# The router's bias, copied by ScalarE into the PSUM banks in place of two bias matmuls per plane

## The chip, the cores and the metric

The kernel runs on one core of one Trainium2 chip. A core has TensorE (PE, matmuls; PEld is its weight load), VectorE (DVE), ScalarE (ACT), GpSimd (POOL) and SyncE (SP, here only a queue that issues DMAs). The engines run at the same time and wait for each other by semaphores. PE writes its products to PSUM, eight banks of 512 fp32 columns on 128 partitions; ACT and DVE can read and write PSUM. The metric is the device time of one execution in microseconds (us).

## What is computed

The input is x, 4096 tokens of 512 values. A first layer (an adaptor per subject and a gated FFN with ternary weights) gives `x1`; a linear layer with a low-rank adaptor gives `h`. The last layer is a mixture whose router chooses two experts of eight for each token and each of the 512 output channels:

```
logits = (h @ router_w.T + router_b).reshape(T, O, E)
probs = softmax(logits);  w, sel = top_k(probs, 2);  w = w / sum(w)
c = zeros((T, E)).at[t_idx, sel].add(w)
expert_out = einsum('th,eoh->teo', h, expert_w) + expert_b
final = einsum('te,teo->to', c, expert_out)
```

The change concerns `+ router_b`, one value for each channel and expert.

## The kernel before

The program has three stages, one after the other. In the first, PE makes `x1` and `h` in 8 blocks of 512 tokens; `h` is written to HBM as a high and a low part (fp32 split in two for the precision of fp32r). The router stage takes 32 tiles of 128 tokens, the expert stage the same 32 tiles once more.

**Router stage.** A tile has two halves `s` of 256 channels (`HO`), a half has four planes `b`, and a plane is one PSUM bank with the logits of 128 tokens, 256 channels and two experts. `router` on PE makes a plane in this way: wait for `evac` (the bank's old contents are read), two products that put the bias into the bank (line 1248: `pick` is a 64-row matrix that selects the rows of one expert, `bias_mm` holds the bias's high part in rows 0 to 7 and its low part in rows 32 to 39), then twelve products of 512 columns (lines 1251 to 1253: four parts `c` of the depth, each high x high, low x high, high x low). The last one counts up `plane_filled`. Behind plane 1 of each half PE runs `codes` for the half before the last: eight products of 256 columns that turn eight sign maps into one code (line 1231); they wait for `signs`.

**ACT** (`router`, `evacuate`, `stand`) takes each filled bank to `L` in SBUF (line 649). Behind the fourth plane of a half stands `stand` of the half before: Sign and Relu over 2048 elements (lines 657, 659), which wait for `tour` and give `signs`. ACT executes in order.

**DVE** (`half`) starts when all four planes of a half are in `L`: it finds the first and second largest of eight (lines 945 to 963), subtracts the second from all (968, 969, counted as `tour`), and in between decodes the code of the half before (909, 913, 918), for which it waits for `code_done`. In the last tiles of the stage (27 to 30) it also sums the weights of tiles 0 and 1, two sums per half (line 1001).

**SP** loads the next tile's `h` (`load_h`) and stores the results.

**Start of the stage.** When the first stage's last gate product is drained, SP loads the bias and then the router's weights, 8 x 1 MB (lines 384 to 387). ACT splits each weight (`split_router`, line 620: high part), DVE makes the low part. On ACT the first split stands ahead of the `x1` store and of the two `turn` copies, for which PE's `adapt` (line 1164) waits by way of DVE. ACT and DVE also split the bias (633, 634, 892), POOL builds `pick`. PE may start plane 0 when the weights of its two experts are split; ACT's first evacuation stands behind its last split.

**End of the stage.** `eraw`, the experts' weights, lies where the router's did, so each pair of loads waits for a plane of the last half. ACT and DVE split them, DVE three of them ahead of its last `half` (line 1024).

The order of every engine's instructions is written out by hand. The part of the code that the change touches:

Of the kernel before, what the change touches and what calls it, by code (L numbers as in the profile page):

```python
# [20 lines left out]
F32 = mybir.dt.float32  # L21
F32R = mybir.dt.float32r
# [3 lines left out]
ALU = mybir.AluOpType  # L26
# [81 lines left out]
def build(nc, x, idx7, idx6, cond_w, w_ffn, WcT, AT, Bt, scal, rwT, rb, ewT, eb, out):  # L108
# [6 lines left out]
    with root:  # L115
        def sb(name, shape, dt, ctx=root):
            return ctx.enter_context(nc.sbuf_tensor(name, shape, dt))
# [71 lines left out]
        p2 = ExitStack()  # L189
        HO = D // 2  # L190

        bias_mm = sb("bias_mm", [64, D], F32R, p2)
        pick = sb("pick", [64, E, P], F32R, p2)
        scratch = ExitStack()
        bias_raw = sb("bias_raw", [64, D], F32, scratch)
        pick_f = sb("pick_f", [64, E, P], F32, scratch)
        scratch.close()
        wts = sb("wts", [P, 2, 2, D], F32, p2)
        pow_id = sb("pow_id", [P, E, P], BF16, p2)
        one_col = sb("one_col", [P, 1], F32, p2)  # L200
# [72 lines left out]
        rhi = sem("rhi")  # L273
        rlo = sem("rlo")
        braw_in = sem("braw_in")
        bzero = sem("bzero")
        bhi = sem("bhi")
        blo = sem("blo")
        b_const = sem("b_const")
        pick0 = sem("pick0")  # L280
        pick_ready = sem("pick_ready")
        hb_in = [sem("hb_in0"), sem("hb_in1")]
        plane_filled = sem("plane_filled")
        evac = sem("evac")
# [60 lines left out]
        def _(sp):  # L345
# [35 lines left out]


            sp.wait_ge(drained, use(NBLK - 1, f"gu{HC - 1}")[0] + 1)
            sp.dma_start(bias_raw[0:E, :], rb).then_inc(braw_in, 16)
            sp.dma_start(bias_raw[32:32 + E, :], rb).then_inc(braw_in, 16)
            for e in range(E):
                sp.dma_start(rraw[:, e, :, :], RWT[e]).then_inc(rraw_in[e], 16)
                if e == 3:
# [75 lines left out]
        @block.gpsimd  # L464
        def _(pool):
            nc.gpsimd.iota(adapter_i[:, :], pattern=[[0, 1]], base=0, channel_multiplier=1).then_inc(consts, 1)
            nc.gpsimd.memset(ident[:, :], 0.0).then_inc(ident_ready, 1)
            pool.wait_ge(ident_ready, 1)
            nc.gpsimd.affine_select(out=ident[:, :], in_=ident[:, :], compare_op=ALU.not_equal, fill=1.0,
                                    base=0, pattern=[[-1, P]], channel_multiplier=1).then_inc(ident_ready, 1)  # L470
            nc.gpsimd.memset(minus_half[:, :], -0.5).then_inc(ident_ready, 1)
            pool.wait_ge(ident_ready, 3)

            def power(i):
                pool.wait_ge(drained, use(i + 1, "ss")[0] + 1)
# [10 lines left out]
            pool.wait_ge(drained, use(NBLK - 1, f"gu{HC - 1}")[0] + 1)  # L486
            nc.gpsimd.memset(pick_f[:, :, :], 0.0).then_inc(pick0, 1)
            for r in range(2):
                pool.wait_ge(pick0, r + 1)
                nc.gpsimd.affine_select(out=pick_f[:, :, :], in_=pick_f[:, :, :], compare_op=ALU.not_equal, fill=1.0,  # L490
                                        base=-32 * r, pattern=[[-1, E], [0, P]], channel_multiplier=1).then_inc(pick0, 1)
            pool.wait_ge(pick0, 3)
            nc.gpsimd.tensor_copy(pick[:, :, :], pick_f[:, :, :]).then_inc(pick_ready, 1)


        @block.scalar
        def _(act):
# [130 lines left out]
            split_router(2)  # L628
            split_router(3)
            adapt(NBLK - 1)  # L630
            act.wait_ge(braw_in, 32)
            act.wait_ge(bzero, 1)
            nc.scalar.activation(bias_mm[0:E, :], bias_raw[0:E, :], ACT.Copy).then_inc(bhi, 1)
            nc.scalar.activation(bias_mm[32:32 + E, :], bias_raw[32:32 + E, :], ACT.Copy).then_inc(bhi, 1)
            copy_h(NBLK - 1, 0)
            send_h(NBLK - 1, 0)
            copy_h(NBLK - 1, 1)
# [2 lines left out]
            for e in range(5, E):  # L640
                split_router(e)
            act.wait_ge(b_const, 1)
            act.wait_ge(h_stored, 16 * 4 * 2 * NBLK)

            def evacuate(n, s, planes=range(4)):

                for b in planes:
                    act.wait_ge(plane_filled, n * PT + (4 * s + b + 1))
                    nc.scalar.activation(L[:, s, 2 * b:2 * b + 2, :], plane[b][:, :, :], ACT.Copy).then_inc(evac, 1)  # L649

            def stand(n, s):

# [15 lines left out]
            def weigh(n, u, trip):  # L668
# [4 lines left out]
                nc.scalar.activation(wts[:, u, 0, :], lead_in[:, u, :], ACT.Sigmoid).then_inc(w_ready, 1)  # L673
                nc.scalar.activation(wts[:, u, 1, :], lead_in[:, u, :], ACT.Sigmoid, scale=-1.0).then_inc(w_ready, 1)  # L674

            router(0, 0)
            router(1, 1)
            router(2, 0)
# [46 lines left out]
        def _(dve):  # L725
# [152 lines left out]
                                        ALU.subtract).then_inc(rlo, 1)  # L878

            finish(NBLK - 1)  # L880
            nc.vector.memset(bias_mm[:, :].bitcast(F32), 0.0).then_inc(bzero, 1)
            turn(NBLK - 1, 0)
            turn(NBLK - 1, 1)
            split_router(0)
# [6 lines left out]
            dve.wait_ge(bhi, 2)  # L891
            nc.vector.tensor_tensor(bias_mm[32:32 + E, :], bias_raw[32:32 + E, :], bias_mm[32:32 + E, :].bitcast(F32),
                                    ALU.subtract).then_inc(blo, 1)
            split_h(NBLK - 1, 0)
            split_router(3)
            split_h(NBLK - 1, 1)
# [187 lines left out]
        def _(pe):  # L1084
# [134 lines left out]

            pe.wait_ge(drained, A_USES - 1)  # L1220
            pe.wait_ge(b_const, 1 + E)
            pe.wait_ge(blo, 1)
            pe.wait_ge(pick_ready, 1)

            def codes(n, s):

# [8 lines left out]
            def router(n, u, trip, first=False):  # L1235
                for s in range(2):
                    o = slice(s * HO, (s + 1) * HO)
                    for b in range(4):
                        if s == 0 and b == 0:
                            pe.wait_ge(hb_in[u], trip * 16 + 16)  # L1240
                        if first and s == 0 and b == 2:
                            pe.wait_ge(drained, A_USES)
                        if first and s == 0:
                            pe.wait_ge(rlo, 2 * b + 2)
                        else:
                            pe.wait_ge(evac, n * PT + (4 * s + b - 3))
                        for r in range(2):
                            mm(plane[b][:, r, :], pick[:, 2 * b + r, :], bias_mm[:, o], start=(r == 0), stop=False)  # L1248
                        w = slice(2 * b, 2 * b + 2)
                        for c in range(DC):  # L1250
                            mm(plane[b][:, :, :], hb[:, u, c, 0, :], rw_hi[:, w, c, o], start=False, stop=False)  # L1251
                            mm(plane[b][:, :, :], hb[:, u, c, 1, :], rw_hi[:, w, c, o], start=False, stop=False)  # L1252
                            last = mm(plane[b][:, :, :], hb[:, u, c, 0, :], rw_lo[:, w, c, o], start=False, stop=(c == DC - 1))  # L1253
# [77 lines left out]
```

## Time and profile before

| | us |
|---|---|
| median of 3 runs | 2628.39 |
| lowest, highest | 2623.78, 2628.57 |
| span of the profiled execution | 2620.5 |
| busy in it: PE, DVE, ACT, POOL | 2539.7, 1777.4, 808.8, 13.0 |
| first plane product, last plane product (start) | 972.5, 1898.9 |

For the profiled execution the page gives only the span, from its first to its last instruction; no time of its own is given. Busy shares say how much an engine has to do, not whether it is waited for; PE's products overlap in the pipeline, so that a product of 0.39 us can start 0.23 us behind the one before. What a plane costs is therefore read from start to start.

### The profile page before, as it was taken

What the parts mean: (1) busy time and instruction counts of PE and PEld (TensorE: products, weight loads), DVE (VectorE), ACT (ScalarE), POOL (GpSimd) and SP (SyncE); (2) the same over time, 40 slices, a digit from 0 to 9 for tenths busy, and PEclk for the clock granted to TensorE, in tenths of its full rate; (3) what the DMA queues carried; (4) which work ended last, traced back from release to release, by engine and by line L of the source; (5) the groups of instructions that cost most, each with busy time, mean ns of one, the idle gap of its engine ahead of it and who ended that gap; (6) DMA issues with size and microseconds to landing.
All of it is one profiled execution on the core that took longest, in us unless ns stands there. A gap on an engine that the chain in (4) does not pass through costs nothing.

```text
span 2620.5 us, 31962 instructions
## 1 busy us (share of the span) xinstructions
PE 2539.7 (97%) x11312; PEld 2004.8 (77%) x11312; DVE 1777.4 (68%) x2719; ACT 808.8 (31%) x984; POOL 13.0 (0%) x20
## 2 busy tenths in 40 slices
PE   5799999999999989999999999999979999999999
PEld 3578888888888867777777777777768888888887
DVE  7973433434344356666676767668889999999995
ACT  5642332323233243434444444444430000000000
POOL 0000000000000000000000000000000000000000
PEclk9999999999999999999999999999989999999999
DMA  4221112111120151111001000100252222222220
GB/s 139 89 93 33 50 32 66 53 45 50 32 66 32 48 183 34 49 40 40 32 32 47 33 32 32 48 32 32 90 181 74 72 72 72 73 74 73 72 73 27
DMA packets 102054, 160.45 MB, mean 61 GB/s; under 512 B 11634, under 2 KB 44914, under 8 KB 101890
## 3 DMA queue, kind: packets, MB, share of 16 engines
q1 hardware_dynamic: 51378, 103.37, 11.5%
q10 hardware_dynamic: 50640, 56.63, 6.7%
q8 instruction: 18, 0.29, 0.0%
q14 instruction: 18, 0.15, 0.0%
HBM read 109.64 MB, written 50.33 MB: 61 GB/s over the span
## 4 chain that ended last, share of the span: by engine, by line
PE 93%; DVE 3%; ACT 1%; issue 1%; SPq 1%; DMA 1%; ACTq 0%; POOL 0%; DVEq 0%; POOLq 0%
PE slot L1125 17%; PE plane L1251 11%; PE plane L1252 9%; PE plane L1253 9%; PE pj L1135 8%; PE ex L1284 8%; PE ex L1286 8%; PE ex L1285 8%; PE plane L1248 4%; PE slot L1175 3%; PE code L1231 2%; PE slot L1101 1%; PE slot L1164 1%; PE slot L1154 1%; DVE acc L1045 0%
## 5 line engine op out<-in xcount | busy, mean ns | idle before, releaser
L1251 PE MATMUL plane<-rw_hi,hb 128*128 128x512 f32 x1024 | 429.7, 420 | 0.0
L1284 PE MATMUL ex<-ew_hi,hb 128*128 128x512 f32 x1024 | 401.1, 392 | 12.8 <-DVE ew_lo L1024 10.4
L1125 PE MATMUL slot<-y_hi,wgu 128*128 128x512 f32 x1024 | 403.5, 394 | 9.6 <-ACT wpj L526 9.6
L1252 PE MATMUL plane<-rw_hi,hb 128*128 128x512 f32 x1024 | 401.4, 392 | 0.0
L1125 PE MATMUL slot<-y_lo,wgu 128*128 128x512 f32 x1024 | 400.8, 391 | 0.0
L1285 PE MATMUL ex<-ew_hi,hb 128*128 128x512 f32 x1024 | 400.1, 391 | 0.0
L1286 PE MATMUL ex<-ew_lo,hb 128*128 128x512 f32 x1024 | 400.1, 391 | 0.0
L1253 PE MATMUL plane<-rw_lo,hb 128*128 128x512 f32 x1024 | 399.9, 390 | 0.0
L649 ACT ACTIVATE L<-plane 128x512 f32<-128x512 f32 x256 | 151.4, 592 | 522.3 <-PE plane L1253 522.1
L1001 DVE SCALAR_TENSOR_TENSOR lead_in<-code_in,wts 128x1024 bf16<-128x1024 bf16 x256 | 311.2, 1216 | 1.2 <-ACT wts L674 0.2
L789 DVE TENSOR_TENSOR hid<-gate,slot 128x512 f32<-128x512 f32 x128 | 87.9, 687 | 259.2 <-ACT gate L535 259.0
L1251 PEld LDWEIGHTS plane<-rw_hi,hb 128*128 128x128 f32 x1024 | 192.3, 188 | 67.7 <-issue 0.2
L1284 PEld LDWEIGHTS ex<-ew_hi,hb 128*128 128x128 f32 x1024 | 193.4, 189 | 54.7 <-issue 9.9
L1125 PEld LDWEIGHTS slot<-y_hi,wgu 128*128 128x128 f32 x1024 | 193.7, 189 | 52.9 <-issue 5.0
L1253 PEld LDWEIGHTS plane<-rw_lo,hb 128*128 128x128 f32 x1024 | 192.8, 188 | 43.8
L1125 PEld LDWEIGHTS slot<-y_lo,wgu 128*128 128x128 f32 x1024 | 193.4, 189 | 40.4
L1285 PEld LDWEIGHTS ex<-ew_hi,hb 128*128 128x128 f32 x1024 | 193.5, 189 | 40.2
L1286 PEld LDWEIGHTS ex<-ew_lo,hb 128*128 128x128 f32 x1024 | 193.2, 189 | 40.5
L1252 PEld LDWEIGHTS plane<-rw_hi,hb 128*128 128x128 f32 x1024 | 193.0, 188 | 31.4
L1135 PE MATMUL pj<-wpj,hid_hi 128*128 128x512 f32 x512 | 206.4, 403 | 1.9 <-DVE hid_lo L795 1.9
L945 DVE TENSOR_TENSOR top<-L 128x1024 f32<-128x1024 f32 x64 | 78.4, 1225 | 187.0 <-ACT L L649 187.0
L673 ACT ACTIVATE wts<-lead_in 128x512 f32<-128x512 f32 x32 | 20.2, 632 | 598.0 <-DVE lead_in L1001 583.1
(122 smaller groups left out, 3323.1 us busy)
## 6 DMA issues: line engine op xcount, KB each, us to landing
hb<-h_scratch SPq DMA_DIRECT2D x34, 512.0 KB, 3.3
h_scratch<-ht ACTq DMA_DIRECT2D x64, 256.0 KB, 3.1
hb<-h_scratch ACTq DMA_DIRECT2D x30, 512.0 KB, 3.8
q_raw<-in_w_ffn SPq DMA_DIRECT2D x24, 512.0 KB, 3.5
x_mix<-in_x SPq DMA_DIRECT2D x8, 1024.0 KB, 5.3
x_scratch<-x_res ACTq DMA_DIRECT2D x8, 1024.0 KB, 4.4
rraw<-in_rwT SPq DMA_DIRECT2D x8, 1024.0 KB, 8.0
lead_scratch<-lead SPq DMA_DIRECT2D x32, 256.0 KB, 2.0
```

The source lines that it names most:

```text
L649: nc.scalar.activation(L[:, s, 2 * b:2 * b + 2, :], plane[b][:, :, :], ACT.Copy).then_inc(evac, 1)
L789: nc.vector.tensor_tensor(hid[:, j % 2, :], gate[:, j % 2, :], slot[s % 2][:, 1, :], ALU.mult).then_inc(drained, 1)
L1001: nc.vector.scalar_tensor_tensor(lead_in[:, k % 2, :].bitcast(BF16).rearrange("p (a n) -> p a n", a=2), code_in[:, k % 2, :, :], float(2 * ...
L1125: last = mm(slot[s % 2][:, g, :], wgu[:, c, r * P:(r + 1) * P], y[:, c, :], start=(c == 0 and v == 0), stop=(c == DC - 1 and v == 1))
L1135: last = mm(pj[k][:, :], h[:, j % 2, k * P:(k + 1) * P], wpj[:, j, :], start=(j == 0 and v == 0), stop=(j == HC - 1 and v == 1))
L1248: mm(plane[b][:, r, :], pick[:, 2 * b + r, :], bias_mm[:, o], start=(r == 0), stop=False)
L1251: mm(plane[b][:, :, :], hb[:, u, c, 0, :], rw_hi[:, w, c, o], start=False, stop=False)
L1252: mm(plane[b][:, :, :], hb[:, u, c, 1, :], rw_hi[:, w, c, o], start=False, stop=False)
L1253: last = mm(plane[b][:, :, :], hb[:, u, c, 0, :], rw_lo[:, w, c, o], start=False, stop=(c == DC - 1))
L1284: mm(ex[e][:, :], hb[:, u, c, 0, :], ew_hi[:, e, c, :], start=(c == 0), stop=False)
L1285: mm(ex[e][:, :], hb[:, u, c, 1, :], ew_hi[:, e, c, :], start=False, stop=False)
L1286: last = mm(ex[e][:, :], hb[:, u, c, 0, :], ew_lo[:, e, c, :], start=False, stop=(c == DC - 1))
```

## The change

ACT fills each bank with the bias before PE comes to it, and all twelve products of a plane add onto it.

- The bias is laid out by the host for all 128 partitions, `[128, 2, 8, 256]` fp32, 2 MB. SP loads it to `bias_sb` with one DMA, ahead of the router's weights, where two of 16 KB were.
- `bias_mm`, `pick` and what makes them (one memset and one subtraction on DVE, two copies on ACT, four instructions on POOL) are gone.
- `evacuate` on ACT reads a bank, waits for its own completion (`evac`), and calls `seed`, a copy of 128x512 from `bias_sb` into the same bank, for the other half of the tile. The last half has no seed.
- PE waits for `seeded` where it waited for `evac`; no product of a plane has `start=True` any more.
- The first four seeds stand on ACT behind all its splits of the router's weights.
- `dynamic_dma_scratch_size` falls to 2048, which makes room in SBUF for `bias_sb`.

```
-            sp.dma_start(bias_raw[0:E, :], rb).then_inc(braw_in, 16)
-            sp.dma_start(bias_raw[32:32 + E, :], rb).then_inc(braw_in, 16)
+            sp.dma_start(bias_sb[:, :, :, :], rb).then_inc(braw_in, 16)
...
+            def seed(s, b):
+                nc.scalar.activation(plane[b][:, :, :], bias_sb[:, s, 2 * b:2 * b + 2, :], ACT.Copy).then_inc(seeded, 1)
             def evacuate(n, s, planes=range(4)):
                 for b in planes:
                     act.wait_ge(plane_filled, n * PT + (4 * s + b + 1))
                     nc.scalar.activation(L[:, s, 2 * b:2 * b + 2, :], plane[b][:, :, :], ACT.Copy).then_inc(evac, 1)
+                    if not (isinstance(n, int) and n == NT - 1 and s == 1):
+                        act.wait_ge(evac, n * PT + (4 * s + b + 1))
+                        seed(1 - s, b)
...
+            act.wait_ge(drained, A_USES - 1)
+            seed(0, 0)
+            seed(0, 1)
+            act.wait_ge(drained, A_USES)
+            seed(0, 2)
+            seed(0, 3)
+            act.wait_ge(h_stored, 16 * 4 * 2 * NBLK)
             router(0, 0)
...
                         if first and s == 0:
                             pe.wait_ge(rlo, 2 * b + 2)
-                        else:
-                            pe.wait_ge(evac, n * PT + (4 * s + b - 3))
-                        for r in range(2):
-                            mm(plane[b][:, r, :], pick[:, 2 * b + r, :], bias_mm[:, o], start=(r == 0), stop=False)
+                        pe.wait_ge(seeded, n * PT + (4 * s + b + 1))
```

PE, in the loop over the tiles, at the end of plane 1 with the codes and the start of plane 2. Before:

```order
L1251 MATMUL plane1<-rw_hi,hb 128x512
L1252 MATMUL plane1<-rw_hi,hb 128x512
L1253 MATMUL plane1<-rw_lo,hb 128x512
L1227 REGISTER_ALU
L1231 MATMUL code1<-sgn,pow_id 128x256 [waits code_read,signs]
L1231 MATMUL code1<-sgn,pow_id 128x256 x7
L1246 REGISTER_ALU
L1248 MATMUL plane2<-bias_mm,pick 128x256 [waits evac]
L1248 MATMUL plane2<-bias_mm,pick 128x256
L1251 MATMUL plane2<-rw_hi,hb 128x512
L1252 MATMUL plane2<-rw_hi,hb 128x512
```

Now:

```order
L1231 MATMUL plane1<-rw_hi,hb 128x512
L1233 MATMUL plane1<-rw_hi,hb 128x512
L1235 MATMUL plane1<-rw_lo,hb 128x512
L1211 REGISTER_ALU
L1215 MATMUL code1<-sgn,pow_id 128x256 [waits code_read,signs]
L1215 MATMUL code1<-sgn,pow_id 128x256 x7
L1228 REGISTER_ALU
L1231 MATMUL plane2<-rw_hi,hb 128x512 [waits seeded]
L1233 MATMUL plane2<-rw_hi,hb 128x512
L1235 MATMUL plane2<-rw_lo,hb 128x512
```

The two bias products between the codes and plane 2 are gone, and the wait for `evac` is one for `seeded` on the first product itself.

ACT, in the same loop, at the last two planes of a half and the `stand` that follows. Before:

```order
L649 ACTIVATE L<-plane2 128x512 [waits plane_filled]
L648 REGISTER_ALU
L649 ACTIVATE L<-plane3 128x512 [waits plane_filled]
L653 ISA
L655 ISA [waits tour]
L657 ACTIVATE sgn<-L 128x2048 [waits code_done]
L658 ISA
L659 ACTIVATE sgn<-sgn,one_col 128x2048 [waits signs]
```

Now:

```order
L628 REGISTER_ALU
L629 ACTIVATE L<-plane2 128x512 [waits plane_filled]
L623 ACTIVATE plane2<-bias_sb 128x512 [waits evac]
L628 REGISTER_ALU
L629 ACTIVATE L<-plane3 128x512 [waits plane_filled]
L623 ACTIVATE plane3<-bias_sb 128x512 [waits evac]
L636 ISA
L638 ISA [waits tour]
L640 ACTIVATE sgn<-L 128x2048 [waits code_done]
L641 ISA
L642 ACTIVATE sgn<-sgn,one_col 128x2048 [waits signs]
```

Between each evacuation and what followed it there is now a copy into the bank that waits for the evacuation; Sign and Relu stand behind the fourth of them.

ACT, at the start of the stage, from the split of expert 5's weights. Before:

```order
L572 DMA h_scratch<-ht 128x4x128 x3
L620 ACTIVATE rw_hi<-rraw 128x2048 [waits rraw_in5]
L620 ACTIVATE rw_hi<-rraw 128x2048 [waits rraw_in6]
L620 ACTIVATE rw_hi<-rraw 128x2048 [waits rraw_in7]
L649 ACTIVATE L<-plane0 128x512 [waits plane_filled,h_stored,b_const]
L649 ACTIVATE L<-plane1 128x512 [waits plane_filled]
L649 ACTIVATE L<-plane2 128x512 [waits plane_filled]
```

Now:

```order
L600 ACTIVATE rw_hi<-rraw 128x2048 [waits rraw_in5]
L600 ACTIVATE rw_hi<-rraw 128x2048 [waits rraw_in6]
L600 ACTIVATE rw_hi<-rraw 128x2048 [waits rraw_in7]
L623 ACTIVATE plane0<-bias_sb 128x512 [waits drained,braw_in,b_const]
L623 ACTIVATE plane1<-bias_sb 128x512
L623 ACTIVATE plane2<-bias_sb 128x512 [waits drained]
L623 ACTIVATE plane3<-bias_sb 128x512
L629 ACTIVATE L<-plane0 128x512 [waits plane_filled,h_stored]
L623 ACTIVATE plane0<-bias_sb 128x512 [waits evac]
```

The four first seeds stand behind the last split, and PE's plane 0 waits for the first of them.

## Rows read from the trace of the kernel before

**Rows 1.** The page: shares, by engine, of the chain of work that ended last.

```profile
PE 93%; DVE 3%; ACT 1%; issue 1%; SPq 1%; DMA 1%; ACTq 0%; POOL 0%; DVEq 0%; POOLq 0%
```

**Rows 2.** Windows: length, us busy by engine (instructions), granted clock, DMA share, GB/s.

```profile
1300.00:1500.00 200.00, 200.00 (x891) 146.81 (x890) 136.95 (x222) 84.01 (x83) 0.00 (x0) 1.00 0.10 37
```

**Rows 3.** The page's groups: one activation of 128x512 that reads and writes SBUF.

```profile
L673 ACT ACTIVATE wts<-lead_in 128x512 f32<-128x512 f32 x32 | 20.2, 632 | 598.0 <-DVE lead_in L1001 583.1
```

**Rows 4.** Order of time, PE, router stage: start, us, engine, line, operation.

```profile
1507.06 0.50 PE L1248 MATMUL plane<-bias_mm,pick 64*128 64x256 f32 x2
1507.49 0.50 PE L1251 MATMUL plane<-rw_hi,hb 128*128 128x512 f32 x1
1507.83 0.40 PE L1252 MATMUL plane<-rw_hi,hb 128*128 128x512 f32 x1
...
1510.12 0.39 PE L1253 MATMUL plane<-rw_lo,hb 128*128 128x512 f32 x1
1510.43 0.50 PE L1248 MATMUL plane<-bias_mm,pick 64*128 64x256 f32 x2
```

**Rows 5.** Order of time, PE, expert stage: the first product of two experts in a row.

```profile
2203.54 0.39 PE L1284 MATMUL ex<-ew_hi,hb 128*128 128x512 f32 x1
...
2206.26 0.39 PE L1284 MATMUL ex<-ew_hi,hb 128*128 128x512 f32 x1
```

**Rows 6.** Order of time, PE: code products before a bias product, and before an expert's.

```profile
1502.69 1.05 PE L1231 MATMUL code<-sgn,pow_id 128*128 128x256 bf16 x8
1503.67 0.50 PE L1248 MATMUL plane<-bias_mm,pick 64*128 64x256 f32 x2
...
1905.67 1.03 PE L1231 MATMUL code<-sgn,pow_id 128*128 128x256 bf16 x8 [0.82 <-issue]
1906.46 0.48 PE L1284 MATMUL ex<-ew_hi,hb 128*128 128x512 f32 x1
```

**Rows 7.** Order of time, ACT, router stage: last evacuation of a half, Sign, Relu.

```profile
1510.54 0.60 ACT L649 ACTIVATE L<-plane 128x512 f32<-128x512 f32 x1 [2.78 <-PE plane L1253]
1511.03 1.90 ACT L657 ACTIVATE sgn<-L 128x2048 bf16<-128x2048 f32 x1
1512.97 2.00 ACT L659 ACTIVATE sgn<-sgn,one_col 128x2048 bf16<-128x2048 bf16 x1
```

**Rows 8.** Order of time, DVE, router stage: one half with two sums, and the next.

```profile
1770.37 1.23 DVE L945 TENSOR_TENSOR top<-L 128x1024 f32<-128x1024 f32 x1 [3.24 <-ACT L L649]
...
1777.38 0.42 DVE L909 TENSOR_SCALAR digits<-code 128x256 int32<-128x256 int32 x1 [1.23 <-PE code L1231]
...
1781.17 0.43 DVE L918 TENSOR_SCALAR slot_code<-digits 128x512 uint16<-128x512 uint16 x1
...
1784.77 1.23 DVE L945 TENSOR_TENSOR top<-L 128x1024 f32<-128x1024 f32 x1 [0.76 <-ACT L L649]
```

**Rows 9.** Order of time, ACT and then PE, start of the router stage.

```profile
946.06 1.91 ACT L620 ACTIVATE rw_hi<-rraw 128x2048 fp32r<-128x2048 f32 x1 [5.22 <-DMA rraw<-in_rwT]
...
979.72 5.51 ACT L620 ACTIVATE rw_hi<-rraw 128x2048 fp32r<-128x2048 f32 x3 [2.71 <-issue]
...
954.03 0.47 PE L1164 MATMUL slot<-x1t_hi,a_hi 128*128 128x512 f32 x1 [2.46 <-DVE x1t_lo L826]
...
984.10 0.76 PE L1248 MATMUL plane<-bias_mm,pick 64*128 64x256 f32 x2 [4.75 <-DVE rw_lo L877]
...
992.94 0.50 PE L1248 MATMUL plane<-bias_mm,pick 64*128 64x256 f32 x2
```

**Rows 10.** Windows at the start of the stage.

```profile
944.00:948.00 4.00, 0.00 (x0) 0.00 (x0) 2.84 (x5) 1.91 (x1) 3.43 (x4) 0.98 1.05 401
...
984.00:988.00 4.00, 3.90 (x10) 3.03 (x11) 4.00 (x2) 2.31 (x3) 0.00 (x0) 0.50 0.15 46
```

**Rows 11.** Order of time, PE and then DVE, end of the router stage.

```profile
1898.91 0.39 PE L1253 MATMUL plane<-rw_lo,hb 128*128 128x512 f32 x1
...
1903.99 1.22 DVE L945 TENSOR_TENSOR top<-L 128x1024 f32<-128x1024 f32 x1
```

More of the change, by code:

```diff
@@ L190, in build @@
         HO = D // 2
[L192 to L197, printed above, removed]
+        bias_sb = sb("bias_sb", [P, 2, E, HO], F32, p2)
         wts = sb("wts", [P, 2, 2, D], F32, p2)
@@ L275, in build @@
         braw_in = sem("braw_in")
-        bzero = sem("bzero")
-        bhi = sem("bhi")
-        blo = sem("blo")
         b_const = sem("b_const")
-        pick0 = sem("pick0")
-        pick_ready = sem("pick_ready")
+        seeded = sem("seeded")
         hb_in = [sem("hb_in0"), sem("hb_in1")]
@@ L483, in _ @@
             power(NBLK - 1)
-            pool.wait_ge(drained, use(NBLK - 1, f"gu{HC - 1}")[0] + 1)
-            nc.gpsimd.memset(pick_f[:, :, :], 0.0).then_inc(pick0, 1)
-            for r in range(2):
[L489 to L493, printed above, removed]
         @block.scalar
@@ L630, in _ @@
             adapt(NBLK - 1)
[L631 to L634, printed above, removed]
             copy_h(NBLK - 1, 0)
@@ L642, in _ @@
             act.wait_ge(b_const, 1)
-            act.wait_ge(h_stored, 16 * 4 * 2 * NBLK)
+            act.wait_ge(braw_in, 16)
+            def seed(s, b):
+                nc.scalar.activation(plane[b][:, :, :], bias_sb[:, s, 2 * b:2 * b + 2, :], ACT.Copy).then_inc(seeded, 1)
             def evacuate(n, s, planes=range(4)):
@@ L880, in _ @@
             finish(NBLK - 1)
-            nc.vector.memset(bias_mm[:, :].bitcast(F32), 0.0).then_inc(bzero, 1)
             turn(NBLK - 1, 0)
@@ L890, in _ @@
                 nc.vector.tensor_scalar(pow_id[:, e, :], ident[:, :], float(2 ** (E - e)), None, ALU.mult).then_inc(b_const, 1)
-            dve.wait_ge(bhi, 2)
-            nc.vector.tensor_tensor(bias_mm[32:32 + E, :], bias_raw[32:32 + E, :], bias_mm[32:32 + E, :].bitcast(F32),
-                                    ALU.subtract).then_inc(blo, 1)
             split_h(NBLK - 1, 0)
@@ L1221, in _ @@
             pe.wait_ge(b_const, 1 + E)
-            pe.wait_ge(blo, 1)
-            pe.wait_ge(pick_ready, 1)
             def codes(n, s):
@@ L1240, in router @@
                             pe.wait_ge(hb_in[u], trip * 16 + 16)
-                        if first and s == 0 and b == 2:
-                            pe.wait_ge(drained, A_USES)
                         if first and s == 0:
                             pe.wait_ge(rlo, 2 * b + 2)
-                        else:
-                            pe.wait_ge(evac, n * PT + (4 * s + b - 3))
-                        for r in range(2):
-                            mm(plane[b][:, r, :], pick[:, 2 * b + r, :], bias_mm[:, o], start=(r == 0), stop=False)
+                        pe.wait_ge(seeded, n * PT + (4 * s + b + 1))
                         w = slice(2 * b, 2 * b + 2)
                         for c in range(DC):
-                            mm(plane[b][:, :, :], hb[:, u, c, 0, :], rw_hi[:, w, c, o], start=False, stop=False)
-                            mm(plane[b][:, :, :], hb[:, u, c, 1, :], rw_hi[:, w, c, o], start=False, stop=False)
-                            last = mm(plane[b][:, :, :], hb[:, u, c, 0, :], rw_lo[:, w, c, o], start=False, stop=(c == DC - 1))
+                            mm(plane[b][:, :, :], hb[:, u, c, 0, :], rw_hi[:, w, c, o], start=False, stop=False,
+                               skip_group_check=True)
+                            mm(plane[b][:, :, :], hb[:, u, c, 1, :], rw_hi[:, w, c, o], start=False, stop=False,
+                               skip_group_check=True)
+                            last = mm(plane[b][:, :, :], hb[:, u, c, 0, :], rw_lo[:, w, c, o], start=False, stop=True,
+                                      skip_group_check=True)
                         last.then_inc(plane_filled, 1)
@@ L1316 @@
         "rwT": g["L1_ffn_router_w"].reshape(D, E, D).transpose(2, 1, 0).reshape(D, E * D),
-        "rb": g["L1_ffn_router_b"].reshape(D, E).T,
+        "rb": np.broadcast_to(g["L1_ffn_router_b"].reshape(1, 2, D // 2, E).transpose(0, 1, 3, 2), (P, 2, E, D // 2)),
         "ewT": g["L1_ffn_expert_w"].transpose(2, 0, 1).reshape(D, E * D),
@@ L1320 @@
     }
-    nc = bacc.Bacc("TRN2", target_bir_lowering=False, num_devices=1)
+    nc = bacc.Bacc("TRN2", target_bir_lowering=False, num_devices=1, dynamic_dma_scratch_size=2048)
     arrays, args = {}, []
```

## Prediction

> **What bounds the kernel now.** Read first the page's chain of work that ended last: 93% of the span is PE [rows 1]. Then the busy time by stretch, for one inside the router stage (about 973 to 1899 us): PE is busy 200 of 200 us at a granted clock of 1.00, DVE 137, ACT 84 [rows 2]. So what leaves PE's stream there shortens the program until another engine or a wait takes over. A busy PE is not a PE at its peak, so I read PE in order of time.
>
> Between the first bias product of one plane and that of the next lie 3.37 us: 0.43 for the two bias products, 0.34 to the second real product, then steps of 0.23 and 0.31 before the next bias product [rows 4]. In the expert stage the same twelve products of 512 columns, bank after bank, with a wait on DVE at each bank, take 2206.26 - 2203.54 = 2.72 us, 0.2267 each [rows 5]. The bias products are 64x128 by 64x256, two for each of 256 planes [rows 4]. So they and the breaks around them cost 3.37 - 2.72 = 0.65 us per plane, far more than their columns.
>
> A half of a token tile is four planes and one group of eight code products: 14.40 us from one DVE start to the next [rows 8]. The stage is 64 such halves; the first two have no codes.
>
> **Removed on PE.** Four planes without bias take 48 x 0.2267 = 10.88 us. The code group stays. In front of a bias product it lasts 0.98 us, in front of a 512-column product 0.79 [rows 6], and the first step behind a break is 0.34, not 0.23 [rows 4]. I take 0.79 + 0.11 = 0.90, since the new successor is a 512-column product; the upper bound is 1.09. A half becomes 11.78 us (bound 11.97).
>
> By the Trainium skill (TensorE: Matmul & The Clock Gate, "Back-to-back issue gap") a product of 256 columns takes 262 cycles, 0.109 us. By that, two per plane over 256 planes are worth 56 us in all. The rows say 0.65 x 256 = 166 us; the page leaves out what the switch of shapes costs, unless that cost stays at the plane's edge (rival C).
>
> **Added on ACT.** Each evacuation is followed by a wait on its own completion and a copy of 128x512 from SBUF into the bank. No row shows ACT or DVE writing PSUM. The nearest rows are the evacuation itself, 0.60 us [rows 7], and the 128x512 activation from SBUF, 0.63 [rows 3]; the own-completion wait is like that between Sign and Relu, 1511.03 + 1.90 to 1512.97 = 0.04 [rows 7]. I take 0.62 + 0.04, and 0.60 to 1.1 for the range. ACT then does 8 x 0.6 + 3.9 + gaps, about 9 us of 11.8: no bound by its sum. A plane's seed is done about 9 us before PE is back at it, so `seeded` is not the late wait.
>
> The late one is at the codes. Let T be the start of the last product of plane 3 (1510.12 in [rows 4]). The evacuation starts at T+0.43, the seed at T+1.07, Sign 0.52 later at T+1.59, where it was T+0.91 [rows 7], and Relu ends at T+5.53. PE reaches the code group after two planes, at T + 25 x 0.2267 = T+5.67. Before, Relu ended at T+4.85 [rows 7] and PE was there at T+7.0 (1502.69 [rows 6] and a half of 14.40). So the slack of 2.1 us shrinks to 0.14, about what a semaphore takes. I add 0.07: **a half is 11.85 us**, 2.55 less. Each 0.1 us more in the seed costs 0.1 us per half, 6 us in all.
>
> The Trainium skill (ScalarE: Activation LUTs, "Step-by-step: what each stage is for") says that ScalarE to PSUM is faster than to SBUF. If so, the seed ends sooner and the 0.07 goes, 4 us; no run of before shows it.
>
> **DVE.** Its half takes 1781.17 + 0.43 less 1770.37 = 11.2 us, of which 1.23 is a wait for the codes [rows 8]: 9.95 of work. It comes to the codes at T+6.8, when PE has just finished them. 9.95 < 11.85, so DVE hides, with 1.9 us to spare. But in the last tiles it also adds up the weights of tiles 0 and 1, two per half in eight halves: 14.40 less the waits of 0.76 and 1.23 is 12.41 us of work [rows 8]. There it falls 0.56 us behind per half, 4.5 in all, 2.6 beyond the slack. DVE's last write to L lies before 1781.17 [rows 8], so without lateness at T+10.6 at the latest, and Sign reads it at T+13.4: 2.8 us of slack, so PE isn't held. The end of the stage is (below).
>
> **The start of the stage.** Two things get later.
> (1) SP's queue now holds a 2.1 MB load where two of 16 KB were, ahead of the eight router weight loads. At the 401 GB/s that flowed there [rows 10] it takes 5.2 us, so ACT's first split moves from 946.06 [rows 9] to 951.3. Behind it on ACT are the store of x1 and the two `turn` copies; they now end the wait of PE's `adapt`, which started at 954.03 after 2.46 us idle [rows 9]: 951.3 + 1.9 + 0.4 for issuing the store + a copy of 128x1024 on ACT (about 1.0, between the 0.60 and 1.90 of [rows 7]) + two subtractions on DVE (1.23 each at 128x1024 [rows 8]) gives 957.1, 3.1 later. The longer idle time costs some clock; I take 3.5 for all that follows, 0 to 6 for the range.
> (2) Before, PE did planes 0 and 1 before its wait of 4.75 us and began plane 2 at 984.10 [rows 9]. Now plane 0 waits for a seed that stands behind all of ACT's splits, which ended at 979.72 + 5.51 = 985.2 [rows 9]; with 3.5 and one seed, PE starts at 989.4. Planes 2 and 3 took 992.94 - 984.10 = 8.84 us [rows 9] where 6.75 is normal: 2.1 of it is the clock, granted at 0.50 in that stretch, 1.2 GHz, after the idle time [rows 10]. Four planes now take 10.88 + 2.1 = 13.0, so half 1 starts at 1002.4, not 992.94: **+9.5 us**. The bias work that DVE and POOL lose lay beside other work: nothing.
>
> **The end of the stage.** The experts hang on DVE's last half, which began at 1903.99, 5.1 us after PE's last plane product at 1898.91 [rows 11]. Ahead of it stand the half before and three splits of 128x2048, about 2.25 each by the 1.23 of 128x1024 [rows 8]. With DVE 2.6 us behind, the half before ends 1.8 us after PE's last product, the three splits end at 8.5: **+3.4 us**, 0 to 6. The expert weights' load starts only a plane or two nearer to the end and is not last. Behind this point nothing is changed.
>
> **Sum.** Half 0: +9.5. Half 1, without codes, from 4 x 3.37 = 13.48 to 10.88: -2.6. Then 62 x 2.55 = -158.1. End: +3.4. Together -147.8 us. The span of the profiled execution, 2620.5, becomes 2472.7; its page gives no other time. The median of the three runs is 7.9 above that span, and I keep this: 2628.4 - 147.8 = **2480.6, say 2481 us**. The smaller SBUF scratch for dynamic DMA costs nothing: all of the kernel's own DMAs are issued by SP and ACT.
>
> **Rivals.**
> A, the forecast: PE's stream bounds, the codes tie. 2470 to 2492. Chance 0.66.
> B, Sign and Relu come late at the codes, because the seed or the wait in front of it costs more than 0.66. For it: there are 0.14 us of slack. Against it: the rows of its kind are narrow, 0.60 to 0.63. At 1.0 us for seed and wait a half is 12.15 and the program takes 2499; at 1.2, 2512. Chance 0.22.
> C, the dead time at a plane's edge belongs to the new bank with its wait, not to the bias products, and only their columns go, 0.2267 per plane. A half is then 14.40 - 4 x 0.2267 = 13.49: 62 x 0.91 = 56, less 11 at the start and 1 at the end, gives 2583. Against it: in the expert stage the banks change with a wait and without a gap [rows 5]. Chance 0.06.
> D, slower: a write of ACT into a bank while PE writes its neighbours is slow, and ACT becomes the bound. Its half is 4 x (0.60 + 0.04 + x) + 3.9; it reaches 14.4 at x = 2.0 us. At 2.2 it is 15.3, 0.9 more over 62 halves: with the start, 2628 + 55 + 12 = 2695. For it: no row of a write to PSUM by ACT. Against it: ACT reads banks beside PE's writes at 0.60. Chance 0.03.
> The rest, 0.03, lies below A: the late start hidden and the end without cost, 2465. That the change doesn't do what it says has next to no room: the order of instructions has lost all 512 bias products.
>
> **How the numbers follow.** The likeliest case is A, 2481. The range takes in A and B, and leaves out C and D: 2468 to 2512. About 0.2% (5 us) is what a measurement of this kernel can tell from no change. Faster: A, B, C and the rest, 0.96. Slower: D, 0.03. Within 0.2%: 0.01, between C and D.
>
> **What would show it.** In the profile of the changed kernel: planes at 2.72 us, halves at 11.8 to 11.9, the seed at 0.6 us, Sign 1.6 us behind T; a wait of the code products for ACT of at most 0.1 us (B: 0.2 or more in each half); no gap at a plane's edge (C: 0.3). PE's first plane near 989 after more than 10 us idle, and DVE without waits in the last eight halves. The forecast fails if a write to PSUM is slower than a read of it, if plane edges keep a gap, or if the start costs over 15 us.

## The result, and the profile after

| | before | after |
|---|---|---|
| median, us | 2628.12 | 2478.09 |
| lowest to highest | 2623.78 to 2628.57 | 2475.09 to 2479.21 |
| runs | 4 | 4 |
| span of the profiled execution | 2620.5 | 2477.3 |

The ratio is 0.9431, 95% interval 0.9419 to 0.9443: 150.0 us less, where 147.8 was forecast.

Below, from the page of after: the shares by engine of the chain that ended last, and the groups of the first plane product and of the seed (idle time before them at the end). Then a window inside the stage, and all that PEld waited for between 1100 and 1700 us.

```profile
PE 88%; DVE 7%; ACT 2%; DMA 1%; issue 1%; SPq 1%; ACTq 0%; POOL 0%; DVEq 0%; POOLq 0%
...
L1231 PE MATMUL plane<-rw_hi,hb 128*128 128x512 f32 x1024 | 406.8, 397 | 12.2 <-ACT plane L623 12.2
...
L623 ACT ACTIVATE plane<-bias_sb 128x512 f32<-128x512 f32 x256 | 153.9, 602 | 8.0
```

```profile
1300.00:1500.00 200.00, 200.00 (x949) 162.89 (x948) 166.80 (x272) 143.51 (x170) 0.00 (x0) 1.00 0.14 47
```

```profile
PEld code L1215 <- ACT sgn L642: 6.8, 26, 0.3
PEld code L1215 <- issue: 6.5, 25, 0.3
```

The chain answers to [rows 1], the window to [rows 2]. PE is still busy all the time, with 949 products in 200 us for 891. PE waited 12.2 us for a seed, all of it at one place, the start of the stage (below). The 256 writes of ACT to PSUM take 0.602 us each, in the mean.

One half of a tile in order of time, first PE, then ACT (start, us, engine, line, operation):

```profile
1501.03 0.39 PE L1235 MATMUL plane<-rw_lo,hb 128*128 128x512 f32 x1
...
1506.47 0.39 PE L1235 MATMUL plane<-rw_lo,hb 128*128 128x512 f32 x1
1506.70 1.05 PE L1215 MATMUL code<-sgn,pow_id 128*128 128x256 bf16 x8
1507.50 0.49 PE L1231 MATMUL plane<-rw_hi,hb 128*128 128x512 f32 x1
1507.83 0.40 PE L1233 MATMUL plane<-rw_hi,hb 128*128 128x512 f32 x1
...
1512.86 0.39 PE L1235 MATMUL plane<-rw_lo,hb 128*128 128x512 f32 x1
```

```profile
1501.45 0.60 ACT L629 ACTIVATE L<-plane 128x512 f32<-128x512 f32 x1 [1.49 <-PE plane L1235]
1502.09 0.60 ACT L623 ACTIVATE plane<-bias_sb 128x512 f32<-128x512 f32 x1
1502.62 1.90 ACT L640 ACTIVATE sgn<-L 128x2048 bf16<-128x2048 f32 x1
1504.55 2.00 ACT L642 ACTIVATE sgn<-sgn,one_col 128x2048 bf16<-128x2048 bf16 x1
```

The last product of plane 3 starts at T = 1501.03, that of the next half at 1512.86: a half is 11.83 us, where it was 14.40. From T to the last product ahead of the codes lie 24 products in 5.44 us, 0.2267 each, over two edges of planes: no gap is left there. ACT's order is that of [rows 7] with the seed in between; Sign starts at T+1.59.

### The profile page after: what moved, and what is told of

Read it like the earlier page. It is cut to its first block, busy times and chain, and to the rows that moved or that the text cites. A ratio compares the mean times of both kernels' runs of the same rounds, so it can differ in the third digit from the quotient of the medians.

```text
span 2477.3 us, 31212 instructions
## 1 busy us (share of the span) xinstructions
PE 2384.1 (96%) x10800; PEld 1950.8 (79%) x10800; DVE 1771.2 (71%) x2717; ACT 958.2 (39%) x1238; POOL 8.9 (0%) x16
## 4 chain that ended last, share of the span: by engine, by line
PE 88%; DVE 7%; ACT 2%; DMA 1%; issue 1%; SPq 1%; ACTq 0%; POOL 0%; DVEq 0%; POOLq 0%
PE slot L1111 18%; PE ex L1267 9%; PE ex L1269 9%; PE ex L1268 9%; PE pj L1121 9%; PE plane L1231 8%; PE plane L1235 8%; PE plane L1233 8%; PE slot L1161 3%; PE code L1215 2%; PE slot L1087 1%; PE slot L1150 1%; DVE lead_in L987 1%; PE slot L1140 0%; DVE top L931 0%
## 5 line engine op out<-in xcount | busy, mean ns | idle before, releaser
L1231 PE MATMUL plane<-rw_hi,hb 128*128 128x512 f32 x1024 | 406.8, 397 | 12.2 <-ACT plane L623 12.2
L1233 PE MATMUL plane<-rw_hi,hb 128*128 128x512 f32 x1024 | 399.7, 390 | 0.0
L515 ACT ACTIVATE gate<-slot 128x512 f32<-128x512 f32 x128 | 76.5, 598 | 367.9 <-PE slot L1111 313.3
```

Source lines behind the costliest of these rows:

```text
L515: nc.scalar.activation(gate[:, j % 2, :], slot[s % 2][:, 0, :], ACT.Silu).then_inc(gate_ready, 1)
```

## Why the bias products were dear

**The price of the bias products by themselves.** The first kernel is the one before without them.

```diff
-                        for r in range(2):
-                            mm(plane[b][:, r, :], pick[:, 2 * b + r, :], bias_mm[:, o], start=(r == 0), stop=False)
...
-                            mm(plane[b][:, :, :], hb[:, u, c, 0, :], rw_hi[:, w, c, o], start=False, stop=False)
+                            mm(plane[b][:, :, :], hb[:, u, c, 0, :], rw_hi[:, w, c, o], start=(c == 0), stop=False)
```

> The kernel before with the 512 bias products left out and nothing in their place; the bias is missing from the logits. ACT, DVE and the DMAs are those of before. If the bias products cost 0.65 us per plane, breaks and all, and the seeds of the changed kernel cost PE's stream nothing, a half is 11.83 us as in the changed kernel and the program takes 2628 - 1.3 (half 0, planes 2 and 3) - 2.6 (half 1) - 62 x 2.57 + 6 (end of the stage, later by as much as in the changed kernel) = 2471, 7 below the changed kernel by its cheaper start. If the seeds hold PE up at the codes, a half here is shorter than 11.83. If the dead time belongs to the plane's edge (rival C), a half is 13.5 and the program takes 2581.

Measured: 2470.44 us (2469.29 to 2471.73), ratio 0.941 (0.9394 to 0.9425), as expected. Its halves take 11.83 us too. So the seeds cost the changed kernel nothing inside the stage. What the changed kernel has more, 7.7 us by the medians, is at the start: its DVE takes up half 0 9.0 us later, counted from the issue of the router's loads (62.60 for 53.58). At the end the two are alike: DVE starts its last half 9.0 us behind PE's last plane product here and 9.1 there, so that lateness comes with the shorter half and not with the seeds.

**Columns, number or rows?** A plane lost 0.65 us with two products of 64 rows and 256 columns. Three kernels change these sizes: the first pads the operands by zero rows to 128 and keeps two products; the second makes one product of 64 rows and 512 columns; the third has both edits, one product of 128 rows and 512 columns. In the last two the bias that is added is not the right one, since both experts of a plane read it from one expert's rows.

```diff
-        bias_mm = sb("bias_mm", [64, D]
+        bias_mm = sb("bias_mm", [P, D]
...
-        pick = sb("pick", [64, E, P]
+        pick = sb("pick", [P, E, P]
```

```diff
-                        for r in range(2):
-                            mm(plane[b][:, r, :], pick[:, 2 * b + r, :], bias_mm[:, o], start=(r == 0), stop=False)
+                        mm(plane[b][:, :, :], pick[:, 2 * b, :], bias_mm[:, :].rearrange("k (a n) -> k a n", a=2), start=True, stop=False)
```

> The kernel before with its bias operands padded with zeros from 64 to 128 rows; still two products of 256 columns per plane. What makes a bias product dear? If it is the switch between 64 and 128 rows, a plane falls from 3.37 to about 2.95 us and the program to 2520. If it is the shortness of the products, behind which the next weight load (0.19) doesn't hide, a plane stays at 3.3 to 3.4 and the program at 2628.

> The kernel before with one bias product of 64 rows and 512 columns per plane in place of two of 256; the bias that it adds is not the right one. If the shortness of the products was dear, a plane falls from 3.37 to 2.95 us (thirteen steps of 0.2267) and the program to 2520. If it was the switch between 64 and 128 rows, the breaks of 0.08 to 0.1 at both edges stay: 3.1 to 3.2 us, 2565 to 2580.

> The kernel before, with the bias as one product of 128 rows and 512 columns in each plane, with the operands padded with zero rows (the two experts of a plane get the same bias, so the bias added is not the right one). It is the fourth corner beside two products of 64 rows (plane 3.37), one of 64 rows (3.35) and two of 128 rows (2.98). Theory rows: a product of 128 rows goes like the other twelve, so the plane is 13 products at 0.2267 = 2.95, the half 4 x 2.95 + 0.90 = 12.7, that is 0.12 per half below two of 128 rows: 2529.1 - 62 x 0.12 = 2522. Rival number: if the second product of the bias cost something of its own beyond its 256 columns (0.11), the plane would fall below 2.95 and the time below 2510.

PE in order of time over one edge of a plane: two products of 128 rows, then one of 64 rows, then one of 128.

```profile
1506.42 0.39 PE L1253 MATMUL plane<-rw_lo,hb 128*128 128x512 f32 x1
1506.65 0.40 PE L1248 MATMUL plane<-bias_mm,pick 128*128 128x256 f32 x2
1506.88 0.40 PE L1251 MATMUL plane<-rw_hi,hb 128*128 128x512 f32 x1
...
1509.63 0.40 PE L1248 MATMUL plane<-bias_mm,pick 128*128 128x256 f32 x2
```

```profile
1512.36 0.39 PE L1252 MATMUL plane<-rw_lo,hb 128*128 128x512 f32 x1
1512.68 0.50 PE L1247 MATMUL plane<-bias_mm,pick 64*128 64x512 f32 x1
1513.11 0.50 PE L1250 MATMUL plane<-rw_hi,hb 128*128 128x512 f32 x1
1513.44 0.39 PE L1251 MATMUL plane<-rw_hi,hb 128*128 128x512 f32 x1
```

```profile
1507.83 0.39 PE L1252 MATMUL plane<-rw_lo,hb 128*128 128x512 f32 x1
1508.06 0.39 PE L1247 MATMUL plane<-bias_mm,pick 128*128 128x512 f32 x1
1508.28 0.39 PE L1250 MATMUL plane<-rw_hi,hb 128*128 128x512 f32 x1
```

| bias products of a plane | plane, us | program, us |
|---|---|---|
| two, 64 rows x 256 columns (before) | 3.37 | 2626.4 |
| one, 64 rows x 512 | 3.35 | 2621.63 (one run) |
| two, 128 rows x 256 | 2.98 | 2529.09 (one run) |
| one, 128 rows x 512 | 2.94 | 2523.68 (2520.75 to 2526.44) |
| none | 2.72 | 2470.44 |

(2626.4 is the median of before beside these runs.) The rows of the operands decide. Of the 0.65 us, 0.23 are the columns, and 0.40 belong to one product of 64 rows between products of 128: the step into it is 0.32 for 0.23, the step out 0.43, the next 0.33. With 128 rows every step is 0.23. That a product is short, or that there are two, costs 0.02 to 0.04. Two expectations were off. For one product of 64 rows 2565 to 2580 was given: it took only 0.16 to 0.2 us for the breaks, where they are 0.40. For two of 128 rows 2520 was given and 2529.09 measured: the plane is 2.98 and not 2.95. The verdict does not hang on these two single runs, since the steps show it plane by plane: the half is 12.82 us with two products of 128 rows, 62 x 1.58 = 98 us less in all, and 14.29 with one of 64. Why PE stops at a change of rows, no run shows.

The Trainium skill (TensorE: Matmul & The Clock Gate, "Back-to-back issue gap") has 0.109 us for 256 columns; two products of 128 rows took 0.23, and here the trace agrees. For products of 64 rows between ones of 128 the same rule is out by a factor of three, and the measurement decides.

So most of the gain was to be had without ScalarE: zero rows beside the bias, on PE, give 97 us (one run, and 98 by its halves) of about 150.

## The tie at the codes

Is ACT just in time? One kernel copies each bias twice, first into a spare bank of PSUM; another puts the seed of plane 3 behind Sign and Relu.

```diff
+                    act.wait_ge(extra, k)
+                nc.scalar.activation(spare[b % 2][:, :, :], bias_sb[:, s, 2 * b:2 * b + 2, :], ACT.Copy).then_inc(extra, 1)
                 nc.scalar.activation(plane[b][:, :, :], bias_sb[:, s, 2 * b:2 * b + 2, :], ACT.Copy).then_inc(seeded, 1)
```

> The changed kernel with a second copy of 128x512 ahead of every seed, from bias_sb into an unused PSUM bank, waiting for the one before it. Theory: Sign and Relu had 0.1 us of slack at the code products, so the 0.55 to 0.6 us that the copy puts in front of them come out at the codes: a half of 12.3 to 12.4 us, PE waits for ACT before each code group, and the program takes 2478 + 62 x 0.5 = 2509 (2503 to 2515). Rival: the slack is larger than that, or the seeds are hidden wholly: 2478 to 2480.

```diff
-                    if not (isinstance(n, int) and n == NT - 1 and s == 1):
+                    if b < 3 and not (isinstance(n, int) and n == NT - 1 and s == 1):
...
+                late(n, 0)
...
+                late(n, 1)
```

(`late` is the wait and the seed of plane 3, as they stood in `evacuate`.)

> The changed kernel with the seed of plane 3 moved behind Sign and Relu. They end 0.65 us earlier, so the slack at the codes grows from 0.1 to 0.75 us. Theory: the tie costs nothing as it stands, halves stay at 11.83 us and the time at 2478. Rival: the tie costs PE a little in each half (the profile names ACT's Relu 26 times as the end of PE's weight-load idle time), then 2472 to 2476.

Measured: 2510.64 us (2509.56 to 2511.58) with two copies, 2478.16 (2477.36 to 2480.67) with the seed behind. PE and then ACT in order of time in the kernel with two copies:

```profile
1503.67 0.39 PE L1239 MATMUL plane<-rw_lo,hb 128*128 128x512 f32 x1
1504.42 1.05 PE L1219 MATMUL code<-sgn,pow_id 128*128 128x256 bf16 x8 [0.35 <-ACT sgn L646]
```

```profile
1510.99 0.60 ACT L633 ACTIVATE L<-plane 128x512 f32<-128x512 f32 x1 [0.89 <-PE plane L1239]
1511.70 0.60 ACT L626 ACTIVATE spare<-bias_sb 128x512 f32<-128x512 f32 x1
1512.23 0.58 ACT L627 ACTIVATE plane<-bias_sb 128x512 f32<-128x512 f32 x1
1512.76 1.90 ACT L644 ACTIVATE sgn<-L 128x2048 bf16<-128x2048 f32 x1
```

From the evacuation to Sign it is 1.77 us for 1.17 (1501.45 to 1502.62), 0.60 more. In the half shown the codes start 0.75 behind the last product for 0.23. In the loop the halves take 12.33 and 12.40 us in turn, so a half is 0.53 longer in the mean. So about 0.07 us were free, and every tenth beyond costs 6 us in all, as rival B had it. The total fits, 62 x 0.53 = 33 us and 32.6 measured, but in part by luck: two halves near the end, behind the four Sigmoids that ACT puts in there, take 13.94, and DVE's last half stands 6.1 behind PE's last product for 9.1, which gives 3.0 back. Between 1100 and 1700 us PEld waited like this with the seed behind, and then in the kernel without bias products or seeds:

```profile
PEld code L1224 <- issue: 13.3, 51, 0.3
```

```profile
PEld code L1231 <- issue: 13.3, 51, 0.3
```

It is 13.3 us in 51 halves in both, and 6.8 + 6.5 = 13.3 in the changed kernel. There "ACT" names, in half of the cases, who came last by a hair, and not a cost.

## The start of the stage

Times here are counted from SP's first issue of the stage's loads. It was at 943.51 us in after, 939.68 in before. PE, then ACT, then PE again in after, in order of time, answering to [rows 9]:

```profile
960.09 0.77 PE L1150 MATMUL slot<-x1t_hi,a_hi 128*128 128x512 f32 x1 [4.82 <-DVE x1t_lo L816]
```

```profile
954.73 1.91 ACT L600 ACTIVATE rw_hi<-rraw 128x2048 fp32r<-128x2048 f32 x1 [10.06 <-DMA rraw<-in_rwT]
...
980.29 1.02 ACT L543 ACTIVATE ht<-slot 128x1024 fp32r<-128x1024 f32 x1 [6.44 <-DMA h_scratch<-ht]
...
985.86 5.51 ACT L600 ACTIVATE rw_hi<-rraw 128x2048 fp32r<-128x2048 f32 x3 [2.75 <-issue]
991.28 2.14 ACT L623 ACTIVATE plane<-bias_sb 128x512 f32<-128x512 f32 x4
```

```profile
992.00 0.77 PE L1231 MATMUL plane<-rw_hi,hb 128*128 128x512 f32 x1 [12.22 <-ACT plane L623]
...
1005.21 0.39 PE L1231 MATMUL plane<-rw_hi,hb 128*128 128x512 f32 x1
```

The first split moved from 6.38 to 11.22, 4.8 later; PE's `adapt` from 14.35 to 16.58, 2.2 later; the last three splits from 40.04 to 42.35, 2.3 later. Half 1 begins at 61.70 for 53.26 [rows 9], 8.4 later. The clock was granted at 0.50 (1.2 GHz) after the 12.22 us without work, as this window of after has it (answering to [rows 10]):

```profile
992.00:996.00 4.00, 4.00 (x10) 3.14 (x11) 2.50 (x2) 1.42 (x3) 0.00 (x0) 0.50 0.02 4
```

Two kernels undo one part each: the bias load goes behind the fourth weight, or the seeds go ahead of the splits of weights 4 to 7.

```diff
-            sp.dma_start(bias_sb[:, :, :, :], rb).then_inc(braw_in, 16)
             for e in range(E):
                 sp.dma_start(rraw[:, e, :, :], RWT[e]).then_inc(rraw_in[e], 16)
                 if e == 3:
+                    sp.dma_start(bias_sb[:, :, :, :], rb).then_inc(braw_in, 16)
```

> The changed kernel with the 2 MB bias load issued behind the fourth router weight instead of ahead of the first. Theory: the load ahead of the weights is what moved ACT's first split by 4.8 us and all that follows on ACT by 2.3; without it the first seed comes 2 us earlier and the program takes 2476 (2474 to 2478). Rival: the shift has another cause, no change.

```diff
             send_h(NBLK - 1, 0)
+            act.wait_ge(braw_in, 16)
+            act.wait_ge(drained, A_USES - 1)
+            seed(0, 0)
+            seed(0, 1)
             copy_h(NBLK - 1, 1)
             split_router(4)
             send_h(NBLK - 1, 1)
+            act.wait_ge(drained, A_USES)
+            seed(0, 2)
+            seed(0, 3)
             for e in range(5, E):
                 split_router(e)
...
-            act.wait_ge(drained, A_USES - 1)
-            seed(0, 0)
-            seed(0, 1)
-            act.wait_ge(drained, A_USES)
-            seed(0, 2)
-            seed(0, 3)
```

> The changed kernel with the first four seeds taken out from behind ACT's splits: two ahead of the second copy of h, two ahead of the splits of experts 5 to 7. Theory: PE's 12.2 us of idle time in front of plane 0 goes, planes 0 and 1 are made at once as before, and only the wait for expert 5's weights is left; half 1 starts about 8.6 - 2 = 6 us earlier, 2472 (2469 to 2475). Rival: PE then waits as long for the weights and nothing is won.

Measured: load later 2478.7 us (2477.92 to 2480.45), no gain, where 2474 to 2478 was expected; seeds early 2472.73 (2472.09 to 2475.71), as expected. The four pieces of the first store of `h`, issued between 970 and 979 us (size, median time from issue to landing), in after, the same with the load later, and then ACT in order of time with the load later:

```profile
h_scratch<-ht ACTq DMA_DIRECT2D x4, 256.0 KB, 3.1
```

```profile
h_scratch<-ht ACTq DMA_DIRECT2D x4, 256.0 KB, 5.0
```

```profile
969.17 1.03 ACT L543 ACTIVATE ht<-slot 128x1024 fp32r<-128x1024 f32 x1 [5.63 <-PE slot L1167]
...
979.62 1.02 ACT L543 ACTIVATE ht<-slot 128x1024 fp32r<-128x1024 f32 x1 [9.42 <-DMA h_scratch<-ht]
```

The first copy of `h` does come 3.3 us earlier (26.0 for 29.3 from the issue). But its store now takes longer, 5.0 us for a piece instead of 3.1, and the second copy, which waits for it, is only 0.3 earlier. The store lies beside the loads of weights 4 and 5: the second of these lands 5.4 us behind the store's first issue, and 1.3 behind it in after. That they are what slows it is the likely reading; no run separates them. PE's plane 0 begins 48.1 behind the issue for 48.5. With the seeds early PE does planes 0 and 1 before the last splits are done, and waits 6.00 us instead of 12.22. Half 1 begins 55.07 behind the issue, 6.6 earlier; the span is only 4.8 shorter from the issue on, since from DVE's last half to the end it is 1.8 longer (720.4 for 718.7), and why is open.

## The end of the stage

After: PE's last plane product, then DVE (the half before the last, three splits, the last half, the first sum of the expert stage).

```profile
1749.53 0.39 PE L1235 MATMUL plane<-rw_lo,hb 128*128 128x512 f32 x1
```

```profile
1742.21 1.22 DVE L931 TENSOR_TENSOR top<-L 128x1024 f32<-128x1024 f32 x1
...
1752.03 6.69 DVE L1010 TENSOR_TENSOR ew_lo<-eraw,ew_hi 128x2048 fp32r<-128x2048 f32 x3
1758.63 1.22 DVE L931 TENSOR_TENSOR top<-L 128x1024 f32<-128x1024 f32 x1
...
1790.32 0.75 DVE L1031 SCALAR_TENSOR_TENSOR acc<-eb_sb,c_ring,xin 128x512 f32<-128x512 f32 x1 [2.92 <-DMA eb_sb<-in_eb]
```

DVE starts its last half 9.1 us behind PE's last product, where it was 5.1 [rows 11]: the half before the last ends 2.5 behind that product, and the three splits stand behind it. To take that away, one kernel spreads the sixteen sums over sixteen halves.

```diff
-            for n in range(NT - 5, NT):
+            for n in range(NT - 9, NT):
...
-                    for t, e in sums[:2]:
+                    for t, e in sums[:1]:
```

> The changed kernel with the 16 sums of tiles 0 and 1 spread over 16 halves, one in each, instead of two in each of eight. Theory: DVE then needs 9.95 + 1.27 = 11.2 us per half, less than PE's 11.83, doesn't fall behind, and the last half of DVE starts 6 us behind PE's last product, not 9.1: 2475 (2473 to 2477). Rival: the experts' weights or the codes end last there, no change.

Measured: 2477.76 us (2476.12 to 2480.85), which the timed runs can't tell from 2478.09; 2473 to 2477 was expected. In its trace the last half starts at 1757.42, 6.4 behind PE's 1751.06, and from the loads' issue (945.10) to the end the span is 1530.7 for 1533.8, 3.1 shorter. What seems to hide it is the first stage, which all kernels have in common: in this profile it took 1.6 longer. Windows of the first 100 us of before and of this kernel; the clock is the third number from the right:

```profile
0.00:100.00 100.00, 62.21 (x241) 44.61 (x242) 82.99 (x119) 60.12 (x72) 0.81 (x8) 0.93 0.37 123
```

```profile
0.00:100.00 100.00, 61.49 (x223) 44.13 (x224) 80.14 (x115) 59.43 (x70) 0.81 (x8) 0.88 0.36 120
```

Over the profiles of all kernels here, the loads' issue comes at 939.7 to 941.3 us in the three with a clock of 0.93 there, at 942.7 and 942.9 with 0.91, at 943.2 to 944.8 in the four with 0.90 (after is one), at 944.8 to 945.3 in the three with 0.88 or 0.89, and at 946.4 with 0.86. These are almost 7 us that no edit made, and they go with the clock granted at the program's start. One kernel's own runs show the like: seven runs of before took 2623.88 to 2629.06 us, at mean clocks of 0.989 to 0.986.

**All together.** Seeds early and sums spread, with the load later and without.

> The changed kernel with three edits together: bias load behind the fourth weight, seeds ahead of the splits of weights 4 to 7, VectorE's sixteen sums one to a half. From the spans of the single ones against the changed kernel, counted from the issue of the router's loads: seeds early -4.8, sums spread -3.1, load later 0 (there the store of the hidden state took the 3 us back). If they add: 2478.1 - 7.9 = 2470. Against: with the load later the seeds may wait for the bias (it landed 18.1 us after its issue there), but that is 963.8 and the seeds come at 975, so no loss is expected.

> The same without the later load. If the later load is worth nothing, this is level with it at 2470 (within 2). If the store of the hidden state is slowed by the load beside it, this one is the faster of the two by 1 to 2.

Measured: with the later load 2472.11 us (2468.31 to 2473.48), without it 2468.86 (2466.53 to 2472.83), ratio to before 0.9405 (0.9392 to 0.9418). The second is the fastest that does the whole work; its times and those of after (2475.09 to 2479.21) have no overlap. DVE starts its last half 6.5 us behind PE's last product (PE, then DVE, in order of time):

```profile
1740.44 0.39 PE L1235 MATMUL plane<-rw_lo,hb 128*128 128x512 f32 x1
```

```profile
1746.90 1.22 DVE L931 TENSOR_TENSOR top<-L 128x1024 f32<-128x1024 f32 x1
```

Whether the later load is worth anything beside the two others stays open: by the medians it costs 3.2 us, by the spans from the issue on (1521.7 for 1523.5) it gains 1.8, and the first stage wanders by more.

## Why the prediction was right

Against the profiled execution of before (2620.5), step by step:

| step | forecast | in the trace |
|---|---|---|
| first stage, unchanged | 0 | +3.8 |
| start, to the begin of half 1 | +9.5 | +8.4 |
| half 1 | -2.6 | -2.5 |
| 62 halves | -158.1 | -159.1 |
| last half of DVE against PE | +3.4 | +4.0 |
| behind it | 0 | +2.2 |
| sum | -147.8 | -143.2 |

- **The half** carries the result, and it held: planes of 2.72, codes at T+5.67, Sign at T+1.59, Relu's end at T+5.52, the seed at 0.60. 11.83 was measured for 11.85. The 0.07 for the tie is the term that was wrong: it is not there with a seed, and 11.83 stands without one too. The 0.05 beyond 11.78 is on PE, where the steps behind the codes are 0.23 to 0.24. One reading was off without an effect: a plane's seed is done 5.4 to 7.7 us before PE is back at the bank, not about 9, since the seeds of planes 0 and 1 stand behind Sign and Relu.
- **The price of a bias product**: 0.65 us was read rightly, from start to start. Its cause was put down to "the switch of shapes". It is the number of rows; a switch from 512 to 256 columns with 128 rows costs nearly nothing. Rival C, a dead time of the bank, fell: no gap at any edge. Rival D fell with the seed's 0.60 us.
- **The start**: part 2, plane 0 behind a seed behind all splits, held (48.5 from the issue for 49.7). In part 1 the size was off: the first split came 4.8 later for 5.2, and PE's `adapt` 2.2 for 3.1. The first copy of `h` did come 3.35 later, but of the 3.5 for all that follows only 2.3 arrived at the last splits: the second copy waits for the store's DMA and not for PE. The low clock cost 2.3 (13.2 us for half 0, 10.88 at full clock), like the 2.1 taken from before.
- **The end**: with DVE 4.0 instead of 3.4 later. The half before the last ends 2.5 behind PE's last product where 1.8 was forecast, and that is the difference.
- **"Behind this point nothing is changed"** was short by 2.2 us. 1.1 of it lies ahead of the first sum of the expert stage: it comes 31.7 behind the last half, 30.6 before, and waits 2.92 us for the DMA of `eb_sb` where it waited 1.72. The kernel without bias products or seeds has 1.9 of the 2.2 too (718.4 us from DVE's last half to the end, for 716.5 before and 718.7 after), so neither the seeds nor the 2 MB load makes most of it. No run was made for the cause of either 1.1.
- **From span to time**: the forecast took its 147.8 off the median of before, and the median came out 2.5 us below it. From the loads' issue to the end, so without the first stage, the spans are 1680.8 and 1533.8: 147.0 less. The medians differ by 150.0, or by 148.3 against the 2626.4 of before beside the later runs. What is left lies within what the first stage wanders by (above). That the sum is right to 1 us is luck in part: start, halves, end and what lies behind it are off by -1.1, -0.9, +0.6 and +2.2, and these cancel.
- **ScalarE to PSUM.** The copy into a bank took 0.602 us, where the forecast had 0.62. The Trainium skill (ScalarE: Activation LUTs, "Step-by-step: what each stage is for") holds the write to PSUM to be faster than one to SBUF. The trace agrees in the direction: the nearest copy of 128x512 from SBUF to SBUF in the same profile, `hid_hi<-hid`, took 0.631, but it writes fp32r, so the pair is not a clean one. The 0.03 us buy nothing here, since PE bounds the half.

## What to carry to other kernels

Read what a small product costs from the start of its neighbours, not from its own columns; if it has fewer rows than they have, pad it with zero rows before anything else is moved. When an engine gets work in the shadow of another, find the one wait with the least slack (here about 0.07 us of 11.83) and double the new work once: the slope tells how near the bound is. After a gain in the middle, look at both ends of the stage, where a load or a queue position can give part of it back. And the change rests on one thing that the runs show for this case alone: products without `start=True` add onto what ACT wrote, in banks that products of the first stage had filled before, and in which no product has `start=True` during the stage. No run has a bank of another history, so try that first where you copy the change.

## What was not expected

- One product of 64 rows between products of 128 costs about 0.40 us beyond its columns (plane 3.35 against 2.94), more than its columns cost.
- The group of eight bf16 code products, of 128 rows, leaves the same mark on one side: the step behind the first product after it is 0.33 us (1507.50 to 1507.83) for 0.23. The forecast had its size (0.11), read from the step behind the bias products.
- A load moved to a later place in the queue made the wait for the store of `h` 9.42 us long instead of 6.44.
- The same first stage took 939.7 to 946.4 us up to the same instruction, along with a mean granted clock of 0.93 to 0.86 in its first 100 us.
